# Two recurrent layers, first layer: expert products that come out turned from copied weights, and score tiles handed on by bank

## What is computed

```python
xn = _layernorm(x)
Q = xn @ Wq.T + bq;  K = xn @ Wk.T + bk;  V = xn @ Wv.T + bv
attn = where(causal, Q @ K.T / sqrt(128), -inf)        # 2048 x 2048
s = softmax(attn) @ V
y = _layer_norm(xn + mha(xn), g1, be1)                 # batch of sequences of length one
idx = argmax(y @ Wg.T)                                 # one of 8 experts per token
h = relu(y @ W1[e] + b1[e])                            # width 512, e = idx of the token
f = _layer_norm(y + h @ W2[e] + b2[e], g2, be2)
x = x + s * silu(f)
```

## Time and profile before

| | us |
|---|---|
| median of 3 runs | 808.08 |
| the profiled execution, its own time | 811.75 |
| its span, first to last instruction | 809.6 |
| expert part, first product to the next scores | 101.99 to 178.27 |
| late attention, scores of tile 9 to output of tile 14 | 178.27 to 251.80 |

### The profile page before, as it was taken

One profiled execution on the slowest core, in us unless ns is written; L12 is line 12 of the kernel. 1 busy time (PEld: TensorE's weight loads), 2 busy tenths in 40 slices (PEclk: granted clock), 3 DMA queues, 4 the chain that ended last, 5 costly groups with the idle time before them and its releaser, 6 DMA issues.

```text
span 809.6 us, 13528 instructions
## 1 busy us (share of the span) xinstructions
PE 675.9 (83%) x4448; PEld 417.0 (52%) x4449; DVE 503.7 (62%) x1196; ACT 326.3 (40%) x498; POOL 317.0 (39%) x339
## 2 busy tenths in 40 slices
PE   3784887877773799988799999999999998689996
PEld 1463656645443546655344444444444434668885
DVE  6563235443545258768777777777787743577776
ACT  0631321213355325545145555556555652222222
POOL 6427000003703333352166767676767674500000
PEclk9988899999878669989789999999999999779999
DMA  9501010100000000000000000000000000000000
GB/s 310 202 0 49 17 40 27 52 26 27 26 1 0 1 1 3 2 2 2 1 1 1 1 0 0 0 0 0 0 0 0 0 1 2 1 0 1 13 13 26
DMA packets 16585, 17.19 MB, mean 21 GB/s; under 512 B 1568, under 2 KB 15008, under 8 KB 16160
## 3 DMA queue, kind: packets, MB, share of 16 engines
q1 hardware_dynamic: 15520, 14.55, 5.3%
q0 software_dynamic: 1024, 2.10, 0.9%
HBM read 11.40 MB, written 5.24 MB: 21 GB/s over the span
## 4 chain that ended last, share of the span: by engine, by line
PE 64%; DVE 19%; issue 6%; ACT 5%; POOL 4%; DVEq 1%; DMA 1%; ACTq 0%
PE ps L1745 10%; PE ps L1723 8%; PE ps L1733 6%; DVE region L964 6%; PE ps L1859 4%; PE ps L1469 3%; PE ps L1542 3%; PE ps L1486 3%; PE ps L1531 2%; PE ps L1643 2%; PE ps L1850 2%; PE ps L1848 2%; PE ps L1849 2%; ACT region L1171 2%; DVE rmax L809 2%
## 5 line engine op out<-in xcount | busy, mean ns | idle before, releaser
L964 DVE TENSOR_REDUCE region<-ps 128x1 f32<-128x512 f32 x256 | 168.4, 686 | 60.9 <-PE ps L1723 60.8
L1305 ACT ACTIVATE region<-ps 128x1024 f32<-128x1024 f32 x128 | 127.1, 1021 | 93.2 <-PE ps L1733 93.2
L1723 PE MATMUL ps<-kr,qmr 96*128 96x512 f32 x256 | 116.2, 461 | 16.5 <-DVE region L964 12.8
L680 POOL TENSOR_TENSOR region<-region 128x512 f32<-128x512 f32 x80 | 106.9, 1338 | 52.8 <-ACT region L1305 51.3
L1733 PE MATMUL ps<-qmr,kr 98*128 98x512 f32 x256 | 110.3, 439 | 3.1 <-ACT region L1305 2.3
L685 POOL TENSOR_TENSOR region<-region 128x512 f32<-128x512 f32 x64 | 82.1, 1283 | 39.2 <-ACT region L1305 34.5
L1745 PE MATMUL ps<-region 128*32 128x512 f32 x512 | 92.0, 599 | 0.1
L1752 PE MATMUL ps<-region,ones 128*32 128x512 f32 x192 | 92.1, 599 | 0.0
L1723 PEld LDWEIGHTS ps<-kr,qmr 96*128 96x128 f32 x256 | 49.7, 195 | 66.1 <-DVE region L964 63.3
L1486 PE MATMUL ps<-region 128*128 128x128 f32 x272 | 43.3, 311 | 40.1 <-ACT region L1181 30.2
L1733 PEld LDWEIGHTS ps<-qmr,kr 98*128 98x128 f32 x256 | 48.8, 193 | 48.7 <-issue 39.7
(11 more groups left out here) (264 smaller groups left out, 1209.9 us busy)
## 6 DMA issues: line engine op xcount, KB each, us to landing
region<-in_w SPq DMA_DIRECT2D x2, 2048.0 KB, 12.9
slots_in<-zeros SPq DMA_DIRECT2D x1, 1536.0 KB, 9.5
region<-slots_in SPq DMA_DIRECT2D x6, 256.0 KB, 2.8
slots_out<-og SPq DMA_DIRECT2D x6, 256.0 KB, 2.4
e<-in_e SPq DMA_DIRECT2D x1, 1152.0 KB, 15.9
x<-in_x SPq DMA_DIRECT2D x4, 256.0 KB, 3.8
out<-y SPq DMA_DIRECT2D x4, 256.0 KB, 2.3
e<-in_e SPq DMA_DIRECT2D x1, 576.0 KB, 16.8
```

The costliest lines, as they stand in the source:

```text
L680: ins = pool.tensor_tensor(o, held(tiles[0]), held(tiles[1]), ALU.add)
L964: dve.tensor_reduce(mxp[:, u // HM, u % HM:u % HM + 1], bank(b), AX.X, ALU.max).then_inc(mx_read, 1)
L1305: act.activation(pm[:, k % HELD, :], ps[:, b:b + 2, :].rearrange("p b c -> p (b c)"), ACT.Exp, scale=SCM).then_inc(p_whole, 1)
L1723: pe.matmul(bank(4 + u % 2 if first else u % 2), qm[0:R_ROWS, parity, h * P:(h + 1) * P], kr[0:R_ROWS, c:c + 512], start=True, stop=True). ...
```

## The change

In the expert part the first product is taken with W1 as the stationary operand and the turned rows as the moving one, in four products of 128 x 128 (new L1569), so that the hidden values come out turned. For that ACT copies the four windows' W1 from the loaded weights to a fixed place, `w1s`, ahead of the products (`weights_copied`, new L1244). Bias and relu are taken by DVE for windows 0 and 2 and by ACT for windows 1 and 3 (`odd_windows`, new L1237). Windows 0 and 1 have their outputs in bank 1, windows 2 and 3 in bank 6, and each pair is handed to DVE by itself.

In the attention the scores signal each bank; DVE takes a maximum per bank and then one over the banks, negated; the scale goes into the queries (`bq_col`, computed on POOL). From tile 8 on the exponentials come in two instructions, the first 1024 columns and the rest, and PE waits for them separately. POOL issues all 16 gathers before the deviations, and the table `after` has `scaled` 0 and 1 one tile later, and `scaled` 2 and 3 too.

```diff
@@ -397,9 +401,9 @@
-                 EARLY + 2: [("added", 2), ("added", 3), ("scaled", 0), ("scaled", 1)],
-                 EARLY + 3: [("inputs", 0), ("inputs", 1), ("scaled", 2), ("scaled", 3)],
-                 EARLY + 4: [("inputs", 2), ("inputs", 3), ("gate", 0), ("gate", 1), ("gate", 2), ("gate", 3)],
+                 EARLY + 2: [("added", 2), ("added", 3)],
+                 EARLY + 3: [("scaled", 0), ("scaled", 1), ("inputs", 0), ("inputs", 1)],
+                 EARLY + 4: [("scaled", 2), ("scaled", 3), ("inputs", 2), ("inputs", 3), ("gate", 0), ("gate", 1), ("gate", 2), ("gate", 3)],
...
@@ -608,11 +614,9 @@
-                if g >= 1:
-                    inverse_deviation(2, g - 1, 1e-5)
-            inverse_deviation(2, NG - 1, 1e-5)
-            for g in range(NG):
-                inverse_deviation(3, g, 1e-5)
+            for n in (2, 3):
+                for g in range(NG):
+                    inverse_deviation(n, g, 1e-5)
...
@@ -802,17 +806,26 @@
-                dve.wait_ge(score_done, i + 1)
                 s = scores_of(i)
-                diag = s[:, P * i:P * (i + 1)]
-                link(dve.tensor_tensor(diag, diag, causal[:, :], ALU.add))
-                link(dve.tensor_reduce(rmax[:, i:i + 1], s, AX.X, ALU.max))
-                dve.tensor_scalar(nmax[:, i:i + 1], rmax[:, i:i + 1], -float(D) ** -0.5, None, ALU.mult).then_inc(nmax_ready, 1)
+                for c in range(banks_of(i)):
+                    dve.wait_ge(score_done, scores_before(i) + c + 1)
+                    if c == i // 4:
+                        diag = s[:, P * i:P * (i + 1)]
+                        link(dve.tensor_tensor(diag, diag, causal[:, :], ALU.add))
+                    some = s[:, 512 * c:min(512 * (c + 1), P * (i + 1))]
+                    if i >= 4:
+                        link.mark(dve.tensor_reduce(rmax[:, i % 2, c:c + 1], some, AX.X, ALU.max))
+                if i >= 4:
+                    link.wait()
+                    some = rmax[:, i % 2, 0:banks_of(i)]
+                dve.tensor_reduce(nmax[:, i:i + 1], some, AX.X, ALU.max, negate=True).then_inc(nmax_ready, 1)
...
@@ -836,19 +849,20 @@
-                for b in range(GROUP):
-                    dve.wait_ge(h_turned, i * GROUP + b + 1)
+                for b in (0, 2):
+                    dve.wait_ge(h_done, i * GROUP + b + 1)
                     for c in range(FC0):
-                        ins = dve.tensor_scalar(hT[:, b, c * P:(c + 1) * P], bank(6 + b % 2)[:, c * P:(c + 1) * P],
+                        ins = dve.tensor_scalar(hT[:, b, c * P:(c + 1) * P], bank(2 + b)[:, c * P:(c + 1) * P],
                                                 b1_col[:, e[b], c:c + 1], 0.0, ALU.add, ALU.max)
-                    ins.then_inc(hT_ready, 1)
-                    if b == 1 and more:
-                        rows_turned(i + 1)
+                    ins.then_inc(even_ready, 1)
+                if more:
+                    rows_turned(i + 1)
                 if not first:
                     dve.wait_ge(og_stored, i * 16)
-                dve.wait_ge(o_done, i + 1)
                 for b in range(GROUP):
-                    dve.tensor_tensor(og[:, b, :], bank(1)[:, b * D:(b + 1) * D], b2_row[:, e[b], :], ALU.add).then_inc(og_ready, 1)
+                    if b % 2 == 0:
+                        dve.wait_ge(o_done, i * 2 + b // 2 + 1)
+                    dve.tensor_tensor(og[:, b, :], bank(1 + 5 * (b // 2))[:, b * D:(b + 1) * D], b2_row[:, e[b], :], ALU.add).then_inc(og_ready, 1)
...
@@ -1161,15 +1179,19 @@
-            def exponents(i):
-                act.wait_ge(nmax_ready, i + 1)
-                if i >= small:
-                    act.wait_ge(d_filled, attention_fill["values", i - 2] + 1)
-                elif i >= 4:
-                    act.wait_ge(d_filled, attention_fill["values", i - 4] + 1)
-                act.activation(prob_of(i), scores_of(i), ACT.Exp, bias=nmax[:, i:i + 1], scale=float(D) ** -0.5,
-                               accum_out=rsum[:, i:i + 1]).then_inc(prob_ready, 1)
+            def exponents(i, piece):
+                a, b = 1024 * piece, min(1024 * (piece + 1), (i + 1) * P)
+                if piece == 0:
+                    act.wait_ge(nmax_ready, i + 1)
...
+                act.activation(prob_of(i)[:, a:b], scores_of(i)[:, a:b], ACT.Exp, bias=nmax[:, i:i + 1],
+                               accum_out=rsum[:, i, piece:piece + 1]).then_inc(prob_ready, 1)
+            pieces_of = lambda i: [(i, piece) for piece in range(2 if i >= small else 1)]
...
@@ -1185,29 +1207,51 @@
-                waiting.append(i)
+                waiting.extend(pieces_of(i))
                 if i < 2 or i == EARLY:
-                    exponents(waiting.pop())
+                    while waiting:
+                        exponents(*waiting.pop(0))
             def value(i):
                 blocks = range(0, i + 1, 4)
                 turned(i, blocks[:2])
+                if waiting:
+                    exponents(*waiting.pop(0))
+                turned(i, blocks[2:3])
                 while waiting:
-                    exponents(waiting.pop(0))
-                turned(i, blocks[2:])
+                    exponents(*waiting.pop(0))
+                turned(i, blocks[3:])
...
-            with act.Fori(0, GROUPS) as i:
+            def odd_windows(i, first=False):
+                e = window_experts(mybir.EngineType.Activation, i)
+                if not first:
+                    act.wait_ge(o_done, i * 2)
+                for b in (1, 3):
+                    act.wait_ge(h_done, i * GROUP + b + 1)
+                    for c in range(FC0):
+                        ins = act.activation(hT[:, b, c * P:(c + 1) * P], bank(2 + b)[:, c * P:(c + 1) * P], ACT.Relu,
+                                             bias=b1_col[:, e[b], c:c + 1])
+                    ins.then_inc(odd_ready, 1)
+            def weights_copied(i):
+                e = window_experts(mybir.EngineType.Activation, i)
                 for b in range(GROUP):
-                    act.wait_ge(h_done, i * GROUP + b + 1)
-                    act.activation(hb[:, b, :], bank(2 + b), ACT.Copy).then_inc(hb_ready, 1)
-            act.wait_ge(o_done, GROUPS)
+                    act.activation(w1s[:, b, :], w1[:, e[b], :], ACT.Copy).then_inc(w1s_ready, 1)
+            act.wait_ge(s_wexp, 64)
+            act.wait_ge(wexp_ready, 1)
+            weights_copied(0)
+            odd_windows(0, first=True)
+            with act.Fori(1, GROUPS) as i:
+                weights_copied(i)
+                odd_windows(i)
+            act.wait_ge(o_done, GROUPS * 2)
...
@@ -1460,20 +1504,22 @@
-                if i >= small:
-                    pe.wait_ge(prob_ready, i)
-                elif i >= 2:
-                    pe.wait_ge(prob_ready, i - 1)
                 for c in range(0, n, 512):
                     m = min(512, n - c)
-                    ins = pe.matmul(scores_of(i)[:, c:c + m], qT[:, P * i:P * (i + 1)], kT[:, c:c + m], start=True, stop=True)
-                ins.then_inc(score_done, 1)
+                    if i > small and c % 1024 == 0:
+                        pe.wait_ge(prob_ready, probs_before(i - 1) + c // 1024 + 1)
+                    elif i == small and c % 1024 == 0:
+                        pe.wait_ge(prob_ready, i - 1 + c // 1024)
+                    elif i >= 2 and c == 0:
+                        pe.wait_ge(prob_ready, i - 1)
+                    pe.matmul(scores_of(i)[:, c:c + m], qT[:, P * i:P * (i + 1)], kT[:, c:c + m], start=True,
+                              stop=True).then_inc(score_done, 1)
             def turn_probs(i, b):
                 k = turns[0]
                 o = a_fill(k)
-                if b == 0:
-                    pe.wait_ge(prob_ready, i + 1)
+                if b % 8 == 0:
+                    pe.wait_ge(prob_ready, probs_before(i) + b // 8 + 1)
...
@@ -1517,38 +1563,37 @@
-            def turn_hidden(i, b):
-                pe.wait_ge(hb_ready, i * GROUP + b + 1)
-                if b >= 2:
-                    pe.wait_ge(hT_ready, i * GROUP + b - 1)
+            def hidden_turned(i, b):
+                pe.wait_ge(w1s_ready, i * GROUP + b + 1)
                 for c in range(FC0):
-                    ins = pe.transpose(bank(6 + b % 2)[:, c * P:(c + 1) * P], hb[:, b, c * P:(c + 1) * P], ident[:, :])
-                ins.then_inc(h_turned, 1)
+                    ins = pe.matmul(bank(2 + b)[:, c * P:(c + 1) * P], w1s[:, b, c * P:(c + 1) * P], xgT[:, b, :],
+                                    start=True, stop=True)
+                ins.then_inc(h_done, 1)
             def second_products(i, b, e):
-                pe.wait_ge(hT_ready, i * GROUP + b + 1)
+                if b % 2 == 0:
+                    pe.wait_ge(even_ready, i * 2 + b // 2 + 1)
+                else:
+                    pe.wait_ge(odd_ready, i * 2 + b // 2 + 1)
                 for c in range(FC0):
```

(20 more changed lines are left out.)

36 lines of the change are left out of this document (26 added, 10 removed).

## The result

The new kernel runs in 786.55 us (median of 4; 783.77 to 789.74), the kernel before in 809.07 beside it (807.72 to 810.26). The ratio is 0.970, with a 95% interval of 0.966 to 0.974, so the time is 2.6 to 3.4% shorter. The forecast was 774.0. The measured time lies outside the forecast's own range (767 to 781) and inside the range for 8 in 10 (764 to 788), near its upper end. The profiled execution took 786.04 us against 811.75, so 25.71 less.

A forecast was written before the change was run, and what follows sets the result against it. Bound by chains of waits: PE and DVE in the experts, scores to product in late attention. 811.75 - 23.2 - 9.4 - 1.5 = 777.7 profiled, 774.0 at the median; own range 767 to 781, 8 in 10: 764 to 788.

The forecast's parts named there:

- Expert part: Six expert groups at 8.4 us instead of 12.44, as wide products, turnings and copies go: -23.2 us.
- the +1.7: Expert part, first group: starts after idle PE at a low granted clock, so 1.7 us is added.
- the +1.0: Expert part, after the last group: PE waits once for DVE, 1.0 us added.
- SP's circle: Expert part: loading the next rows but one behind the previous group's outputs takes 8.0 us a group, just within PE's 8.2.
- rival 1: Expert part: batches start afresh, or a circle over ACT or SP binds; 10.1 us a group, 784 us; chance 0.17.
- Rivals 4 and 5: Expert part: PE at the low clock, 824.5 us, chance 0.04; narrow products dearer in a stream, 808 us, chance 0.02.
- Late attention: From tile 9's scores to output 14: 64.1 us against 73.5, a gain of -9.4 us.
- 16 of them, from about 2.6 on, end at 22.6: Late attention: 16 gathers in us from tile 9's scores, landed before `added` 2 and 3, removing DVE's 5.38 wait.
- rival 3: Early attention: the 8.66 us stop at 73 us changes; gone, 765 us, chance 0.06; grown, 782 us, chance 0.06.
- Rival 2: Late attention: no gain by bank and piece, PE's order unchanged and DVE with more instructions; 780 us, chance 0.10.
- Early attention: Tiles 7 and 8, behind the scatter, have 0.5 and 1.0 us less of maximum: -1.5 us.
- my sign for a mistake, 2 us: After tile 14's output: the forecast is wrong if the second layer's length moves by more than 2 us.

The follow-up runs named there:

- e9: New kernel with POOL waiting for the last four gathers to land before the next four, scatters unbroken: 762.73 us, ratio 0.947 to the kernel before.
- e10: Kernel before with all 16 gathers ahead of the deviations and a POOL wait after every fourth scatter and gather: 796.10 us, ratio 0.990.
- e11: New kernel with POOL waits after every fourth scatter and gather, and `scaled` where the old table had it: 765.50 us, ratio 0.951 to the kernel before.
- e5: New kernel with POOL waiting for the last four transfers to land before the next four, in scatter and gathers: 768.35 us, ratio 0.949 to the kernel before.
- e1: New kernel run and traced once more, no edit: 784.57 us, ratio 0.967 to the kernel before.
- e6: New kernel with one POOL pause after the eighth transfer, in scatter and gathers: 770.97 us, ratio 0.950 to the kernel before.
- e8: New kernel with the old expert part, so the attention change alone: 807.26 us, ratio 0.998 to the kernel before.
- e12: New kernel with POOL waits after every fourth gather, none among the scatters, and the old table of `scaled`: 774.12 us, ratio 0.953 to the kernel before.
- e3: New kernel with POOL's old order, gathers in 8, 4 and 4 with deviations between: 782.40 us, ratio 0.959 to the kernel before.
- e7: Kernel before with the new expert part alone: 785.85 us, ratio 0.971 to the kernel before.

## Why the prediction was right in sign and 12.5 us too low

**Expert part, -28.3 for -23.2: right mechanism, three terms too dear.** The groups take 7.9 to 8.3, 8.0 in the mean, instead of 8.4, which is 2.4 us over six: the register load of 0.34 that I put into PE's sum overlaps with PE's work, and four products cost the 0.89 of the earlier trace rows in the new stream as well. The first group ran at the full clock (2.94 for three batches against 2.69), so the +1.7 stayed away: the granted clock of 101 to 108 us is 1.00 where the earlier trace rows had 0.76, as this row of stages shows (columns as in the earlier trace rows).

```profile
101.00:108.00 7.00, 6.75 (x60) 6.75 (x61) 3.63 (x12) 3.02 (x10) 0.00 (x0) 1.00 0.14 40
```

PE is busy 6.75 of those 7 us and was 6.02 before. The wait after the last group is 0.70 and the missing turning of that group pays for it, so the +1.0 went too. 2.4 + 1.7 + 1.0 are the 5.1. SP's circle, which I had 0.2 under PE's, ended a wait of PE in three groups and cost 0.36 at most; ACT's never did. So rival 1 occurred in its mildest form and without its price. Rivals 4 and 5 did not occur: four narrow products took 0.89 us and a wide one 0.92.

**Late attention, -0.2 for -9.4: the step that failed.** It reads "16 of them, from about 2.6 on, end at 22.6", that is, that 16 gathers in a row only make data come earlier. They did end at 22.3 us, but what they would do to ACT and DVE stands in the sum as nothing. The streams behind it were right to 2 us: without the stops e9 has its scores at 4.9, 12.9, 19.6, 29.8, 40.1 and 50.6 us and output 14 at 63.1, for which the forecast has 4.8, -, -, 27.9, 38.9, 50.6 and 64.1. The runs split the term into four:

| from the old 73.5 to the new 73.4 | us | from |
|---|---|---|
| gathers ahead, without a stop | -9.0 | before, e10 |
| maxima by bank, exponentials in pieces | -4.5 | e10, e11 |
| new table of `scaled` | +3.1 to +4.1 | e11 against e9, e5 |
| the stops of the 16 gathers | +9.3 | after, e5 |

My -9.4 stood for the first three together, a gain of 12.1 less 2.7 for the table; the runs have 13.5 less 3.1 to 4.1 (from tile 15's scores to output 14 I had 13.5; it is 12.5 in e9 and 10.8 in e11). What was missing is the last row of the table. The profile before had a hint of it: the stop of 8.66 that ended with the scatter, another row of 16. I took it for a matter of that place and priced it as rival 3, and did not ask what the new row of 16 would do. Rival 2's 780 was near by its size (6.4 lost of 9.4), for another reason than the one it gives.

**Early attention, -0.7 for -1.5.** From tile 8's scores to the first product it takes 10.9 us instead of 12.0, which is the part of the gain behind the scatter. The rest can't be read from one execution: traced again (e1), the same kernel has its first product at 99.33 instead of 101.25. Rival 3 did not occur in the new kernel, and e5, e6, e9 and e11 show what its "gone" is worth: the first product comes at 91.6 to 94.5 us.

**From output 14 on, +3.2 for 0.** The code is the same. Stages of the kernel before, then of the new one, from output 14:

```profile
251.80:331.00 79.20, 60.03 (x689) 37.87 (x687) 45.31 (x81) 31.54 (x54) 29.36 (x35) 0.78 0.01 1
...
600.00:809.60 209.60, 183.02 (x1022) 126.05 (x1022) 140.35 (x410) 73.58 (x104) 67.36 (x63) 0.94 0.02 6
```

```profile
222.60:302.00 79.40, 60.26 (x690) 38.05 (x687) 45.60 (x82) 31.57 (x55) 29.35 (x35) 0.79 0.00 1
...
571.00:783.60 212.60, 186.63 (x1035) 128.88 (x1033) 142.08 (x412) 75.31 (x106) 67.97 (x64) 0.94 0.02 5
```

The loss is in the last stretch and it is PE's busy time, 3.6 us more. But e1 is the same kernel, and its trace has 557.7 us from output 14 on, with PE busy for 182.7 us in the last stretch, as in the kernel before. So the 3.2 us come with the execution or the chip and not with the change. Over all 14 traces the length goes from 554.6 (e8) to 564.0 (e12), so my sign for a mistake, 2 us, was set too tight.

Together: 777.7 - 5.1 (experts) + 9.2 and + 0.8 (attention) + 3.5 (the end and around) = 786.1 for the profiled 786.04. The other 4.2 of the 12.5 are in the step to the median: the old profiled execution lay 3.67 above it, the new one 0.5 below. That the median lies within the range for 8 in 10 is in part luck: the range was made that wide for rivals 1 and 2, and what filled it was a cost that neither of them names, with 5.1 us of the opposite sign from the experts.

**A better version.** Pauses and the new expert part together beat both kernels in all five forms tried (e5, e6, e9, e11, e12: 0.947 to 0.953). The shortest span of a trace, 759.9 us, is that of e11, pauses after every fourth transfer with the old table, but the traced execution was the fastest of its five. The medians don't show the 3 to 4 us of the table: on the same chip e9 has 762.73 and e11 765.50, where e11 also pays its wait for the last scatters. Which form is best stays open.

## What to carry to other kernels

Before putting indirect transfers of GpSimd in one long row, look in the profile for a stop of other engines that ends with such a row, and try a wait after every few of them: here a wait costs 1.7 us on an engine that has time, and all of them together bring the ratio from 0.967 to 0.949. Where another engine needs the last of the transfers at once, as PE here after the scatter, the waits are paid. Undo the parts of a change of order one by one, since a move that makes data early can hide a gain and a loss of the same size. Where the stationary operand changes with every product anyway, choose the one that spares the turning and the copy behind it.

## What the runs showed of the hardware

Rows of 16 indirect transfers of GpSimd, one every 1.25 us, stopped ScalarE or VectorE: the longest wait in each such row was 7.1 to 14.9 us, with an unknown queue as the releaser. At the gathers they go on 2.8 us after the last issue, at the scatter already about then (ACT at 80.64 and 82.77 in the new kernel, the last scatter issued at 82.11). Rows of eight left stops of 1.9 to 4.7 us in e3 and e6 and none at the eight gathers of the kernel before and of e7; rows of four left none. On one of the chips the 16 scatters stopped nobody (e9), and the kernel before was 0.6 to 1.0% faster there. The untouched code behind output 14 took 557.7 and 561.0 us in two executions of the same kernel. Narrow fp32 products of 128 x 128, each with its own stationary operand, went at 0.89 us per four for whole groups, with the granted clock at 1.00.
